# Half of one group's stacking transfers issued by ScalarE instead of SyncE

## The chip, the core and the metric

The kernel runs on one core of a Trainium2 chip. The metric is the device time of one execution in microseconds, median of the timed executions. The engines named here are TensorE (PE, matrix products), VectorE (DVE), ScalarE (ACT), GpSimd (POOL) and SyncE (SP, which only issues transfers here). SyncE and ScalarE can both issue DMA transfers; each has a queue of its own.

## What is computed

A recommendation tower over 512 samples. 26 table rows per sample are gathered, projected and normalised, mixed to 32 rows and normalised again; with one dense row they give 33 vectors, whose pairwise products (the lower triangle) go through a linear layer, a normalisation, and three top layers:

```python
x = layer_norm(dense_t @ Wd.T, gd, bd)
y = layer_norm(jnp.einsum('bnd,ed->bne', sparse_t, Ws), gs, bs)
y = jnp.einsum('bne,pn->bep', y, Wsi)
y = layer_norm(y, gsi, bsi)
y = jnp.swapaxes(y, 1, 2)
T = jnp.concatenate([x[:, None, :], y], axis=1)
Z = jnp.einsum('bnd,bmd->bnm', T, T)
Zflat = Z[:, TRIL_I, TRIL_J]
out = layer_norm(Zflat @ Wl.T, gl, bl)
...
h = jnp.concatenate([z, r_dense_t], axis=1)
h = jnp.maximum(h @ W_top1 + b_top1, 0.0)
h = jnp.maximum(h @ W_top2 + b_top2, 0.0)
y = h @ W_top3
```

## The kernel before

The samples are worked in four groups of 128 (numbers 0 to 3). A group has 26 tiles of gathered rows, taken in 13 pairs (`combine`, line 438) and, two pairs at a time, in quads (`transposes`, `spread_products`, `embT_copy`, `u_sums`, `u_spread`, `scale_rows`), which normalise the gathered rows. Every group also has four blocks of 32 samples, each in two halves: `c_copy` (line 764, ScalarE) takes the mixed rows out of PSUM, `project` (line 457, TensorE) multiplies them by the weights, `y_square` (line 769, ScalarE) squares the result, `y_sums` (line 1088, VectorE) adds it up, `y_spread` (line 775, ScalarE) takes the root and `normalise` (line 1093, VectorE) writes the normalised rows to `T`. `gram_products` (line 477, TensorE) forms the pairwise products in two halves, and `gram_copy` (line 779, ScalarE) copies each half to the tile `gram`; eight such copies make a group, and each raises the semaphore `gram_ready` by one.

The triangle is then folded so that it fills 128 partitions. `stack` (line 351) does that with sixteen SBUF-to-SBUF transfers of 32 KB each (a from 0 to 3, r from 0 to 3), from `gram` to one of two tiles `z`; SyncE issues all sixteen for groups 0, 1 and 2, after `gram_ready` has reached the group's eight copies and after `f_done` says that the flat layer two groups back has read its tile. Each transfer raises `stacked` by 16, so a group is complete at 256. The last group is folded by copies on ScalarE, VectorE and GpSimd instead.

`merge` (line 1104, VectorE) waits for the 256, turns one half (line 1110) and selects between the halves (line 1113) into `zm`. `flat_layer` (line 491, TensorE) multiplies `zm` by the weights of the linear layer (line 503), then a last step (line 507). Its result is normalised (`z_stats`, `f_spread`, `z_normalised`), transposed, scaled, and goes through the top layers `mlp1`, `mlp2` (line 544; line 549 is its product for groups 0 to 2) and `mlp3`.

Every engine has a list of calls of its own, in a fixed order; engines are tied only by semaphores. Up to about the third group the order comes from a clock of ticks with a lag for each call; from there on the order is written out by hand (lines 660 to 738 for TensorE, 920 to 973 for ScalarE, 1189 to 1227 for VectorE). The calls of ScalarE around the change are lines 931 to 942: `gram_copy(end - 4, 1)`, the last copy of group 2's grams; `c_copy(end - 3)` (line 767), two `u_spread` (line 762), `h1_relu(last - 2)` (line 820), `y_square(end - 3)` (line 772), `y_spread(end - 3)` (line 777), `embT_copy(QUADS - 2)` (line 757), `x_columns(last)` (line 788), `c_copy(end - 2)` (line 767) and `h2_relu(last - 2)` (line 834). `last` is 3 and `end` is 15; block `end - 3` is group 3's first. In VectorE's list `merge(last - 1)`, the merge of group 2, stands behind `normalise(end - 2)`; in TensorE's list group 2's flat layer stands behind `gram_products(end - 2, 1)`.

Of the kernel before, what the change touches and what calls it, by code (L numbers as in the profile page):

```python
# [19 lines left out]
PR = 32  # L20
# [7 lines left out]
NG = B // GROUP  # L28
# [4 lines left out]
QUARTERS = GROUP // QS  # L33
# [4 lines left out]
NB = GROUP // 4  # L38
# [80 lines left out]
def wait_if_any(eng, semaphore, value):  # L119

    if value > 0:
        eng.wait_ge(semaphore, value)


def dlrm_tower(nc, t):
    ctx = ExitStack()
    with ctx:
        def sb(name, shape, dt=F32):
            return ctx.enter_context(nc.sbuf_tensor(name, shape, dt))
# [4 lines left out]
        def sem(name):  # L134
            return ctx.enter_context(nc.semaphore(name))
# [21 lines left out]
        z = [sb(f"z{i}", [P, 2, 4, KC, NB]) for i in range(2)]  # L157
# [93 lines left out]
        f_done = sem("f_done")  # L251
# [20 lines left out]
        gram_ready = sem("gram_ready")  # L272
# [37 lines left out]
        stacked = [sem(f"stacked{i}") for i in range(2)]  # L310
# [11 lines left out]
        def folded(g, a, r, columns):  # L322

            at = PR * (a % 2) + KC * r
            of = gram[PR * a:PR * a + PR, g % 2, at:at + KC, columns]
            row, k, column = of.ap
            return bass.AP(of.tensor, of.offset, [row, (NB * (PR - KC - 2 * KC * r), 2), k, column])

        def layer1(g, m):
            return PF[:, P * m:P * m + P] if g < NG - 1 else [*TU, *(c[:, :, :].rearrange("p b c -> p (b c)") for c in PC)][m][:, 0:P]  # L330
# [9 lines left out]
        @block.sync  # L340
        def _(sp):
            sp.dma_start(index_parts[:, :], t["index_parts"]).then_inc(l_ids, 16)
            sp.dma_start(proj_w[:, :], t["proj_w"]).then_inc(l_proj, 16)
            sp.dma_start(bias9[:, 0:E], t["bs"].partition_broadcast(P)).then_inc(l_nine, 16)
            sp.dma_start(sel9[:, :, :], t["sel9"]).then_inc(l_nine, 16)
            sp.wait_ge(gathered[5], 32)
            for dst, src in ((wl, "wl"), (wlx, "wlx"), (gb, "gb"), (sel, "sel"), (gbsi, "gbsi"), (mask, "mask"),
                             (glbl, "glbl"), (w1, "w1"), (b1, "b1"), (w2, "w2"), (b2, "b2"), (w3, "w3")):
                sp.dma_start(dst[tuple(slice(None) for _ in dst.shape)], t[src]).then_inc(l_late, 16)

            def stack(g, samples):

                sp.wait_ge(gram_ready, g * QUARTERS + samples.stop // SLOTS)
                wait_if_any(sp, f_done, g - 1)
                for a in range(4):
                    for r in range(4):
                        sp.dma_start(z[g % 2][PR * r:PR * r + PR, :, a, :, samples], folded(g, a, r, samples)).then_inc(stacked[g % 2], 16)

            for g in range(NG - 1):
                stack(g, slice(0, NB))  # L360

            sp.wait_ge(y_ready, NG)
            sp.dma_start(t["out"].rearrange("b one -> one b"), y_row[:, :]).then_inc(stored, 16)
            sp.wait_ge(stored, 16)
# [376 lines left out]
        def _(act):  # L741
# [13 lines left out]
            def embT_copy(i):  # L755
                act.wait_ge(t_done, i + 1)
                act.activation(embT[:, i % 2, :], TU[i % NTU][:, 0:QUAD], ACT.Copy).then_inc(embT_ready, 1)  # L757

            def u_spread(i):

                act.wait_ge(u_ms_ready, i + 1)
                act.activation(u_sd[:, i % 2, :], u_ms[:, i % 2, :], ACT.Sqrt).then_inc(u_sd_ready, 1)

            def c_copy(m):
                act.wait_ge(c_done, m + 1)
                wait_if_any(act, y_done, m - 1)
                act.activation(cs[:, m % 2, :, :], PC[m % NPC][:, :, :], ACT.Copy).then_inc(cs_ready, 1)

            def y_square(m):
                act.wait_ge(y_done, m + 1)  # L770
                for half in range(2):
                    act.activation(ysq[:, half, :, :], PY[half][:, :, :], ACT.Square,  # L772
                                   scale=float(PR) ** -0.5).then_inc(ysq_ready, 1)

            def y_spread(m):
                act.wait_ge(y_ms_ready, 2 * m + 2)
                act.activation(y_sd[:, m % 2, :, :], y_ms[:, m % 2, :, :], ACT.Sqrt, bias=eps[:, :]).then_inc(y_sd_ready, 1)

            def gram_copy(m, half):
                g, q = m // BLOCKS, 2 * (m % BLOCKS) + half  # L780
                act.wait_ge(z_done, 2 * m + half + 1)
                wait_if_any(act, stacked[g % 2], STACKING * (g // 2))
                act.activation(gram[:, g % 2, :, SLOTS * q:SLOTS * (q + 1)], PZv,  # L783
                               ACT.Copy).then_inc(gram_ready, 1)

            def x_columns(g):
                wait_if_any(act, z_done, g * QUARTERS)
                act.activation(T[:, :, 2 * PR:2 * PR + 2].rearrange("p (b h) s -> p b h s", h=2),
                               xT[:, GROUP * g:GROUP * (g + 1)].rearrange("p (h s b) -> p b h s", h=2, s=2), ACT.Copy).then_inc(xcol_ready, 1)
# [27 lines left out]
            def h1_relu(g):  # L817
                if g < NG - 1:
                    act.wait_ge(h1_sum_ready, g + 1)
                    act.activation(h1[:, :, :], h1[:, :, :], ACT.Relu).then_inc(h1_ready, 1)  # L820
                else:
                    for m in range(H1 // P):
                        act.wait_ge(m1_done, g + m + 1)
                        act.activation(h1[:, m, :], layer1(g, m), ACT.Relu, bias=b1[:, m:m + 1]).then_inc(h1_ready, 1)
# [22 lines left out]
            def wl5_copy():  # L847
                act.wait_ge(w5_done, 1)
                act.activation(wl5[0:ROWS_X, :], PF[0:ROWS_X, :], ACT.Copy).then_inc(wl5_ready, 1)

            def late_stack(g, samples):

                act.wait_ge(gram_ready, QUARTERS * (g + 1))
                for a, r in ACT_PARTS:
                    i = act.activation(z[g % 2][PR * r:PR * r + PR, :, a, :, samples], folded(g, a, r, samples), ACT.Copy)
                i.then_inc(late_stacked, 1)
# [63 lines left out]
            last = NG - 1  # L920
# [9 lines left out]
            embT_copy(QUADS - 3)  # L930
            gram_copy(end - 4, 1)
            c_copy(end - 3)
            u_spread(QUADS - 4)
            u_spread(QUADS - 3)
            h1_relu(last - 2)
            y_square(end - 3)
            y_spread(end - 3)
            embT_copy(QUADS - 2)
            x_columns(last)
            c_copy(end - 2)  # L940
            h2_relu(last - 2)
# [21 lines left out]
            gram_copy(end, 0)  # L963
            gram_copy(end, 1)
            late_stack(last, slice(EARLY, NB))
            h1_relu(last - 1)
            f_spread(last)
# [332 lines left out]
```

## Time and profile before

| | us |
|---|---|
| median of 3 timed runs | 181.1 |
| lowest and highest of them | 179.42, 181.12 |
| span of the profiled execution, first to last instruction | 216.2 |

The page gives the span of the profiled execution and no time around it. Busy shares of that span: TensorE 75%, VectorE 56%, GpSimd 50%, ScalarE 36%. The granted TensorE clock is 0.865 of full speed over the span. Durations below are those of the profiled execution; the start of its span is 0. An issue of a transfer ("SPq", "ACTq") is the time that the issuing engine spends on it, not the time until the data have landed.

### The profile page before, as it was taken

Reading aid. Unit: us, or ns where it says so; the run is one execution under the profiler, and the core shown is the slowest. Engines: PE = TensorE matmul, PEld = TensorE weight load, DVE = VectorE, ACT = ScalarE, POOL = GpSimd, SP = SyncE. Lnnn points to the kernel's source line nnn. Section 1 sums busy time; section 2 is a strip of 40 time slices with the busy share of each in tenths; the row PEclk is TensorE's granted clock in tenths of the full one; section 3 lists DMA queues with packets and bytes.
Section 4 is the critical chain, followed back from the end, with each engine's and each line's share of the span. In section 5 each row is a group of like instructions: output and inputs, shape, how many; then the busy total and the mean of one; then the engine's idle time right before and its main releaser. Section 6 shows DMA issues by size and latency. Waiting matters only on the chain.

```text
span 216.2 us, 3315 instructions
## 1 busy us (share of the span) xinstructions
PE 163.0 (75%) x1189; PEld 110.3 (51%) x1189; DVE 120.7 (56%) x325; ACT 78.7 (36%) x221; POOL 107.9 (50%) x139
## 2 busy tenths in 40 slices
PE   0373406489859698686699689789969999978985
PEld 0171303354645356444275576385649676448574
DVE  1405200997384445766665818559548689876410
ACT  2103001051546354414424234444233655463152
POOL 4777774571665646667545666656755000352000
PEclk9996555859979799969589959799997999999999
DMA  6211891010111101231001112211101011000000
GB/s 210 82 28 26 270 352 25 12 27 15 18 24 20 27 16 21 52 78 37 18 17 23 26 27 55 70 30 24 25 18 28 19 49 33 0 2 3 0 0 0
DMA packets 9730, 9.76 MB, mean 45 GB/s; under 512 B 3666, under 2 KB 7378, under 8 KB 9459
## 3 DMA queue, kind: packets, MB, share of 16 engines
q0 software_dynamic: 3328, 3.41, 8.1%
q1 hardware_dynamic: 5954, 5.18, 7.6%
q10 hardware_dynamic: 432, 0.97, 1.4%
q8 instruction: 9, 0.15, 0.3%
q14 instruction: 7, 0.05, 0.1%
HBM read 7.98 MB, written 0.00 MB: 37 GB/s over the span
## 4 chain that ended last, share of the span: by engine, by line
PE 45%; another core or an unknown queue 17%; DVE 16%; ACT 10%; issue 9%; DMA 2%; SPq 0%; ACTq 0%; DVEq 0%
PE pz L487 7%; PE pc L451 6%; PE pf L503 5%; PE py L472 4%; PE tu L434 4%; PE pf L529 3%; PE tu L424 3%; PE pf L522 3%; DVE y_ms L1091 3%; ACT gram L783 2%; PE py L503 2%; PE py L467 2%; DMA proj_w<-proj_w_dram 2%; PE pf L605 2%
## 5 line engine op out<-in xcount | busy, mean ns | idle before, releaser
L389 POOL DMA_INDIRECT emb<-tables_dram,rows_at x104 | 100.0, 961 | 61.2 <-PE tu L424 26.4
L487 PE MATMUL pz<-T 128*64 128x67 f32 x512 | 24.4, 242 | 9.7 <-ACT gram L783 4.0
L451 PE MATMUL pc<-wbd,emb 128*128 128x192 f32 (+4 forms) x128 | 30.0, 344 | 1.4 <-issue 1.1
L451 PEld LDWEIGHTS pc<-wbd,emb 128*128 128x128 f32 x128 | 20.7, 206 | 20.1 <-issue 17.1
L487 PEld LDWEIGHTS pz<-T 128*64 128x64 f32 x512 | 19.9, 149 | 18.4 <-issue 12.9
L1091 DVE TENSOR_REDUCE y_ms<-ysq 128x16 f32<-128x512 f32 x32 | 20.4, 679 | 12.6 <-ACT ysq L772 12.4
L757 ACT ACTIVATE embT<-tu 128x256 f32<-128x256 f32 x26 | 9.9, 380 | 43.3 <-PE tu L424 31.0
L434 PE MATMUL tu<-mbd,embT 128*128 128x128 f32 x104 | 19.2, 313 | 3.8 <-issue 2.3
L472 PE MATMUL py<-cs,wg 64*128 64x512 f32 x64 | 21.1, 746 | 0.0
L783 ACT ACTIVATE gram<-pz 128x268 f32<-128x268 f32 x32 | 12.5, 389 | 23.7 <-remote 12.6
L1100 DVE TENSOR_TENSOR T<-py,y_r 128x512 f32<-128x512 f32 x32 | 20.6, 687 | 0.6
L424 PE MATMUL tu<-proj_w,emb 128*128 128x128 f32 x52 | 13.0, 326 | 10.2 <-DMA emb<-tables_dram,rows_at 7.8
L772 ACT ACTIVATE ysq<-py 128x512 f32<-128x512 f32 x32 | 17.3, 594 | 8.7 <-PE py L472 6.3
L434 PEld LDWEIGHTS tu<-mbd,embT 128*128 128x128 f32 x104 | 16.1, 214 | 5.1 <-issue 2.6
L1071 DVE TENSOR_TENSOR prod<-tu,emb 128x256 f32<-128x256 f32 x26 | 10.9, 417 | 13.8 <-issue 7.5
L405 POOL COPY z<-gram 32x128 f32<-32x128 f32 x16 | 4.6, 286 | 22.1 <-ACT gram L783 21.4
L424 PEld LDWEIGHTS tu<-proj_w,emb 128*128 128x128 f32 x52 | 7.1, 159 | 14.3 <-DMA emb<-tables_dram,rows_at 9.2
L1082 DVE RECIPROCAL u_r<-u_sd 128x4 f32<-128x4 f32 x26 | 4.5, 172 | 14.5 <-issue 8.4
L503 PE MATMUL pf<-wl,zm 128*128 128x512 f32 x24 | 11.9, 604 | 0.0
L1085 DVE TENSOR_TENSOR emb<-emb,u_r 128x256 f32<-128x256 f32 x26 | 11.1, 429 | 0.9
L1074 DVE TENSOR_REDUCE u_sum<-prod 128x4 f32<-128x256 f32 x26 | 10.9, 420 | 0.9
L529 PE MATMUL pf<-zT,w 128*128 128x128 f32 x72 | 11.0, 308 | 0.0
(142 smaller groups left out, 208.4 us busy)
## 6 DMA issues: line engine op xcount, KB each, us to landing
emb<-tables_dram,rows_at POOLq DMA_INDIRECT x104, 2.4
z<-gram SPq DMA_DIRECT2D x48, 32.0 KB
w<-w_dram SPq DMA_DIRECT2D x1, 1280.0 KB
wl<-wl_dram SPq DMA_DIRECT2D x1, 1024.0 KB
denseT<-denseT_dram ACTq DMA_DIRECT2D x1, 512.0 KB
w<-w_dram SPq DMA_DIRECT2D x1, 512.0 KB
comb_w<-comb_w_dram ACTq DMA_DIRECT2D x1, 311.0 KB, 3.3
sel<-sel_dram SPq DMA_DIRECT2D x1, 240.0 KB
```

The source lines that it names most:

```text
L389: pool.indirect_dma_start(emb[:, 2 * pair + half, :], None, t["tables"], bass.IndirectOffsetOnAxis(ap=rows_at[:, 2 * g + half, j:j + 1], a ...
L424: mm = pe.transpose(TU[i % NTU][:, P * half:P * half + P], emb[:, 4 * i + 2 * half:4 * i + 2 * half + 2, :].rearrange("p t d -> p (t d)"), ...
L434: mm = pe.matmul(TU[i % NTU][:, QUAD + P * half:QUAD + P * half + P], embT[:, i % 2, P * half:P * half + P], mbd[:, :], start=True, stop=True)
L451: mm = pe.matmul(PC[m % NPC][:, :, :].rearrange("p b c -> p (b c)")[:, col:col + n], of, wbd[:, :, :].rearrange("p b c -> p (b c)")[:, at: ...
L472: mm = pe.matmul(PY[half][:, :, :].rearrange("p b c -> p (b c)"), wg[at, :], cs[at, m % 2, :, :].rearrange("p b c -> p (b c)"), start=Fals ...
L487: mm = pe.matmul(PZ[2 * PR * h:2 * PR * h + 2 * PR, ITEMS * b:ITEMS * (b + 1)], of[:, 0:2 * PR], of, start=True, stop=True)
L503: pe.matmul(f_bank(g)[:, :], zm[g % 2][:, k, :, :].rearrange("p a b -> p (a b)"), wl[:, k, :], start=(k == 0), stop=False)
L529: mm = pe.matmul(layer1(g, m), w1[:, c, P * m:P * m + P], zT[:, c, :], start=(c == 0), stop=(c == 2))
L772: act.activation(ysq[:, half, :, :], PY[half][:, :, :], ACT.Square, scale=float(PR) ** -0.5).then_inc(ysq_ready, 1)
L783: act.activation(gram[:, g % 2, :, SLOTS * q:SLOTS * (q + 1)], PZv, ACT.Copy).then_inc(gram_ready, 1)
L1091: dve.tensor_reduce(y_ms[:, m % 2, half, :], ysq[:, half, :, :], AX_X, ALU.add).then_inc(y_ms_ready, 1)
L1100: dve.tensor_tensor(to, PY[half][:, :, :].rearrange("p (b s) c -> p b s c", s=2), y_r[:, m % 2, half, :].rearrange("p (b s) -> p b s", s=2 ...
```

## The change

SyncE's `stack` gets a third argument, the rows a that it is to issue: all four for groups 0 and 1, rows 0 and 1 for group 2. ScalarE gets a call `stack_row` that waits for the same two semaphores and issues the transfers that it is given; four such calls, of two transfers each, stand in its list for rows 2 and 3 of group 2: behind `c_copy(end - 3)`, `h1_relu(last - 2)`, `y_square(end - 3)` and `embT_copy(QUADS - 2)`. The transfers themselves, their tiles and the count that the merge waits for are as before.

```diff
-            def stack(g, samples):
+            def stack(g, samples, rows):
 
                 sp.wait_ge(gram_ready, g * QUARTERS + samples.stop // SLOTS)
                 wait_if_any(sp, f_done, g - 1)
-                for a in range(4):
+                for a in rows:
                     for r in range(4):
                         sp.dma_start(z[g % 2][PR * r:PR * r + PR, :, a, :, samples], folded(g, a, r, samples)).then_inc(stacked[g % 2], 16)
 
             for g in range(NG - 1):
-                stack(g, slice(0, NB))
+                stack(g, slice(0, NB), range(4) if g < NG - 2 else range(2))
...
+            def stack_row(g, a, ranges):
+
+                act.wait_ge(gram_ready, QUARTERS * (g + 1))
+                wait_if_any(act, f_done, g - 1)
+                for r in ranges:
+                    act.dma_start(z[g % 2][PR * r:PR * r + PR, :, a, :, :], folded(g, a, r, slice(0, NB))).then_inc(stacked[g % 2], 16)
+
...
             c_copy(end - 3)
+            stack_row(last - 1, 2, (0, 1))
             u_spread(QUADS - 4)
             u_spread(QUADS - 3)
             h1_relu(last - 2)
+            stack_row(last - 1, 2, (2, 3))
             y_square(end - 3)
+            stack_row(last - 1, 3, (0, 1))
             y_spread(end - 3)
             embT_copy(QUADS - 2)
+            stack_row(last - 1, 3, (2, 3))
             x_columns(last)
             c_copy(end - 2)
             h2_relu(last - 2)
```

## Rows read from the trace of the kernel before

**Rows 1.** The page's chain that ended last: share of the span by engine.

```profile
PE 45%; another core or an unknown queue 17%; DVE 16%; ACT 10%; issue 9%; DMA 2%; SPq 0%; ACTq 0%; DVEq 0%
```

**Rows 2.** The chain in order of time, 160 to 200: start us, us, what.

```profile
172.19 2.05 PE pf L549 x16
...
183.70 2.77 PE pf L503 x6
```

**Rows 3.** Timeline of SyncE's queue, groups 0 and 2: start us, us, engine, line, what.

```profile
87.12 11.17 SPq L357 DMA_DIRECT2D z<-gram  x16
...
170.08 10.18 SPq L357 DMA_DIRECT2D z<-gram  x16
...
171.36 1.24 SPq L357 DMA_DIRECT2D z<-gram  x2
```

**Rows 4.** Line 357, all its issues: ns min/median/max of one, first and last start us.

```profile
L357 SPq DMA_DIRECT2D z<-gram x48: 585/597/1441, 87.1 to 179.7; - x48
```

**Rows 5.** Windows: stretch, its length, busy us (x) of each engine, clock, DMA share, GB/s.

```profile
170.00:184.00 14.00, 13.64 (x136) 9.55 (x135) 12.33 (x33) 8.26 (x24) 0.00 (x0) 1.00 0.16 39
...
181.00:181.50 0.50, 0.50 (x13) 0.38 (x13) 0.50 (x1) 0.50 (x2) 0.00 (x0) 1.00 0.19 46
181.50:182.00 0.50, 0.50 (x16) 0.43 (x13) 0.50 (x3) 0.12 (x2) 0.00 (x0) 1.00 0.00 0
```

**Rows 6.** Timeline of VectorE, 155 to 200.

```profile
172.76 1.27 DVE L1091 TENSOR_REDUCE y_ms<-ysq 128x16 f32<-128x512 f32 x2
...
180.25 1.29 DVE L1100 TENSOR_TENSOR T<-py,y_r 128x512 f32<-128x512 f32 x2
...
181.54 0.72 DVE L1110 STREAM_SHUFFLE zm<-z 128x512 f32<-128x512 f32 x1
182.29 0.73 DVE L1113 COPY_PREDICATED zm<-mask,z 128x512 f32<-128x512 int32 x1
```

**Rows 7.** Timeline of TensorE's products, 166 to 206.

```profile
175.04 0.64 PE L434 MATMUL tu<-mbd,embT 128*128 128x128 f32 x4
...
176.27 0.39 PE L467 MATMUL py<-bias_r,bias_l 64*128 64x512 bf16 x2
...
183.63 2.84 PE L503 MATMUL pf<-wl,zm 128*128 128x512 f32 x6
```

**Rows 8.** Timelines of ScalarE and SyncE near the start: issues of loads.

```profile
1.16 0.46 ACTq L743 DMA_DIRECT2D wdT<-wdT_dram  x1
...
1.22 0.41 SPq L343 DMA_DIRECT2D proj_w<-proj_w_dram  x1
...
22.66 0.42 SPq L349 DMA_DIRECT2D gb<-gb_dram  x1
...
25.02 0.73 SPq L349 DMA_DIRECT2D mask<-mask_dram  x1
```

**Rows 9.** Timeline of ScalarE, 168 to 204; in brackets: idle before it and its releaser.

```profile
169.67 0.39 ACT L783 ACTIVATE gram<-pz 128x268 f32<-128x268 f32 x1 [0.69 <-PE pz L487]
169.96 0.59 ACT L767 ACTIVATE cs<-pc 128x512 f32<-128x512 f32 x1
...
171.42 0.20 ACT L762 ACTIVATE u_sd<-u_ms 128x4 f32<-128x4 f32 x1 [0.78 <-DVE u_ms L1077]
171.53 0.61 ACT L820 ACTIVATE h<-h 128x512 f32<-128x512 f32 x1
172.05 1.06 ACT L772 ACTIVATE ysq<-py 128x512 f32<-128x512 f32 x2
174.06 0.32 ACT L777 ACTIVATE y_sd<-y_ms,eps 128x32 f32<-128x32 f32 x1 [0.95 <-DVE y_ms L1091]
174.50 0.38 ACT L757 ACTIVATE embT<-tu 128x256 f32<-128x256 f32 x1
174.78 0.42 ACT L788 ACTIVATE T<-xT 128x128 f32<-128x128 f32 x1
175.10 0.59 ACT L767 ACTIVATE cs<-pc 128x512 f32<-128x512 f32 x1
```

## Prediction

> **What bounds the kernel now.** I read the page's chain first: TensorE holds 45% of it, and no share belongs to the queue of the stacking transfers [rows 1]. Then the same chain in order of time around the change. From the second layer of group 1 (line 549, 172.19 us) to group 2's flat layer (line 503, 183.70 us) it runs through TensorE alone, instruction behind instruction [rows 2], and TensorE is busy 13.64 of the 14.00 us from 170 to 184 [rows 5]. So in this stretch a microsecond that TensorE is kept waiting is a microsecond of the end, and a microsecond saved elsewhere is worth nothing unless TensorE waited for it.
>
> Next, the queue that the change unloads. SyncE issues group 2's sixteen transfers from 170.08 on in 10.18 us, so the last issue ends at 180.26 [rows 3]; one issue takes 0.597 us in the median [rows 4] and two take 1.24 us [rows 3]. When has the last one landed? The DMA engines still move 46 GB/s in 181.0 to 181.5 and nothing in 181.5 to 182.0 [rows 5]. And who wants it? VectorE's merge of group 2 (lines 1110 and 1113). It starts at 181.54, which is just where the normalisation ahead of it on VectorE ends (180.25 + 1.29 = 181.54), so VectorE did not stand idle for the stack. It ends at 182.29 + 0.73 = 183.02 [rows 6], and TensorE turns to the flat layer only at 183.63 [rows 7]. The stack is just in time on VectorE, and 0.6 us early on TensorE.
>
> **The part taken from SyncE.** Eight issues instead of sixteen end at 170.08 + 8 x 0.64 = 175.2 us, five microseconds sooner. Nothing stands behind them on SyncE but the wait for the output. The merge stays at its place in VectorE's order, behind the normalisation that ends at 181.54, so an earlier stack starts nothing earlier. Gain: none that the rows show on VectorE, and on TensorE none either, for the 0.6 us of slack lies behind the merge. The data are the same bytes in the same number of transfers; two queues feed the same DMA engines, which are busy for 0.16 of this stretch [rows 5].
>
> **The part given to ScalarE.** No row shows ScalarE issuing an SBUF-to-SBUF transfer. Its price is bounded by two rows: ScalarE's own loads at the head, 0.46 us for one [rows 8], and the same transfers on SyncE, 0.62 us [rows 3]. Same shape is the nearer row: 0.62, a pair 1.24. There are four pairs, so 8 x 0.62 = 5.0 us of ScalarE's instruction stream; the added waits (all grams of group 2 copied, group 0's flat layer done) are satisfied at 170.06, when the last gram copy ends [rows 9], and the other one long before.
>
> What of the 5.0 us is felt depends on whether an issue holds up only the calls behind it, or also waits for the call ahead of it. In the rows a ScalarE call starts 0.1 us before the one ahead ends (the copy of line 767 at 169.96, the gram copy ending at 170.06 [rows 9]), so the engine does not empty between calls. I take it that a pair is issued while the call ahead of it is still running. The walk, with old times in brackets, all from [rows 9] for ScalarE and [rows 7] for TensorE:
>
> - Pair 1: 170.08 to 171.32, beside the copy of line 767. The square roots behind it (line 762) come at 171.34 and 171.45 (the second came at 171.42), so h1_relu ends at 172.17 (172.14): 0.03 late for TensorE.
> - Pair 2: 171.58 to 172.82, beside h1_relu. y_square 172.84 to 173.90 (172.05 to 173.11): 0.8 late. VectorE's two y_sums, 0.64 each, begin at 173.4 (172.76 [rows 6]) and end at 174.7.
> - Pair 3 lies beside y_square and y_sums. y_spread 174.72 to 175.04 (174.06), embT 174.95 to 175.33 (174.50 to 174.88).
> - Pair 4: 174.97 to 176.21. x_columns 176.23, c_copy 176.55 to 177.14 (175.10 to 175.69): 1.45 late.
> - TensorE: spread_products wants embT and starts at 175.37 (175.04), 0.33 late. The projection of line 467 wants c_copy: 177.17 (176.27), 0.9 late. From there everything is 0.9 late together, since ScalarE and VectorE now wait for TensorE, and TensorE has no idle time left in which to catch up before the flat layer, whose length doesn't change.
>
> That is the upper end of this reading: +0.9 us. With 0.44 us for an issue (near the head's 0.46) the same walk puts c_copy's end at 176.38 and the projection at 176.41: +0.14. If the calls behind a pair are also handed to the engine before they can run, so that pairs follow one another without waiting for the calls between them, pair 4 is over at 175.2, c_copy ends at 176.2 and the loss is again about 0.1. No row tells these apart; I take the middle of 0.1 and 0.9, +0.5 us. That uses up the cover: c_copy had 176.27 - 175.69 = 0.58 us of slack before the projection.
>
> The Trainium skill has a rule on just this point: in "Perfetto Trace Analysis", "Per-engine timelines", an activation is pushed into a wait queue and the sequencer goes on, while a DMA instruction occupies the sequencer until its descriptors are made. By it the loss would lie near the lower end; the overlap of 0.1 us in [rows 9] agrees with it, and no row shows an issue among ScalarE's calls.
>
> **The sum against the times.** The span of the profiled execution is 216.2 us; the page gives no time around it. The median of the three timed runs is 181.1, so the profiled execution is 35.1 us longer, and no row says where. I carry the difference over unscaled, since in this stretch TensorE works without gaps at a granted clock of 1.00 [rows 5], that is at 2.4 GHz, and has nothing to be shortened: 216.2 + 0.5 = 216.7 for the span, 181.1 + 0.5 = 181.6 for the median. One per cent is 1.8 us, about what a measurement of this kernel can tell from no change.
>
> **Rivals.**
> 1. Slower: an issue on ScalarE begins only when the call ahead has ended. Then pair 1 runs from 170.55 (end of the copy, 169.96 + 0.59), h1_relu ends at 172.6, pair 2 at 173.85, y_square at 174.9, pair 3 at 176.15, embT at 176.8, pair 4 at 178.05, c_copy at 179.0, and the projection is 2.7 us late: 183.8 us. It decides as soon as c_copy is over 0.58 us late. For it: no row shows an issue beside a running call. Against it: the calls themselves overlap.
> 2. Slower still: two queues that issue at once take turns, so that each issue costs 1.24 us while SyncE has work. Pair 1 ends at 172.56, h1_relu at 173.4, pair 2 at 175.3, pair 3 at 177.8, pair 4 (alone) at 179.3, c_copy at 180.2: 4.0 us late, 185.1 us. Against it: at the head ScalarE's issue of 0.46 us runs beside SyncE's of 0.41, and SyncE alone at 22.66 takes 0.42 [rows 8]. The Trainium skill, "Perfetto Trace Analysis", "DMA Instruction — HWDGE", says that the descriptor generator is shared and locked by one sequencer at a time; by that rule this rival would be the forecast, but the two overlapping issues of [rows 8] speak against any turn-taking that shows at that size.
> 3. Faster: in the timed executions SyncE issues more slowly and the merge does wait. SyncE's issues of 0.73 us exist [rows 8], and group 0's sixteen took 11.17 us [rows 3]. The stack has 0.6 us of slack before TensorE, so it decides from 0.64 + 0.6 / 16 = 0.68 us an issue. At 0.73 the stack lands 16 x 0.09 = 1.5 us later, TensorE waits 0.9, and the change takes that away for 0.1 to 0.5 of its own: 180.3 to 180.7 us. For more than 1% the issue would have to take 0.8. For it: the merge starts within hundredths of the landing. Against it: nothing in the profile makes SyncE slower when it isn't profiled.
> 4. No effect at all: ScalarE's pairs fit wholly into its idle time (0.95 us before y_spread and smaller ones [rows 9]): 181.1. This lies inside the forecast's range.
>
> **How the numbers follow.** The forecast with rival 4: 0.62, own range 181.1 to 182.0. Rival 1: 0.20. Rival 2: 0.06. Rival 3: 0.12. Nearly all of the first and most of the last are within 1%; a scatter of the measurement (179.42 to 181.12 in three runs) moves some of each over the line. Faster by over 1%: 0.11, from rival 3 and the scatter. Within 1%: 0.62. Slower by over 1%: 0.27, from rivals 1 and 2. The range, 179.7 to 184.1, takes in rival 3 with some scatter and rival 1; it leaves out rival 2 and a larger gain.
>
> **What would show it.** Right: SyncE's issues of group 2 end near 175; eight issues stand on ScalarE's queue between 170 and 176.5, some of them while a call is running; h1_relu moves by under 0.1, y_square by up to 0.8 and the projection of line 467 by 0.1 to 0.9 relative to the gram copy at 169.67; the merge still follows the normalisation without a gap; the flat layer is late by what the projection is. Wrong: issues that begin only at the end of a call and a projection late by over 2 us (rival 1); issues of over 1 us on both queues (rival 2); a merge that starts earlier against the normalisation, or a flat layer that comes closer to the gram copy (rival 3).

## The result, and the profile after

The changed kernel takes 181.85 us (median of 22 runs, 180.57 to 184.13) against 181.13 us for the kernel before (22 runs, 179.42 to 182.42). The ratio is 1.0052 with a 95% interval of 1.0031 to 1.0074: 0.0052 x 181.13 = 0.9 us slower, between 0.6 and 1.3; the medians lie 0.72 us apart. Ratios here are formed without the runs that took over 1.5% longer than the fastest of their kernel, medians with them, so the two can differ. The loss lies within the 1% band, and the median inside the forecast's own range (181.1 to 182.0), 0.25 us above the time predicted.

The profiled execution of the changed kernel has a span of 180.9 us, not 216. A second trace of the kernel before (the first experiment) has 180.6. So the two kernels are compared below by a common mark, the start of the last gram copy of group 2, after which ScalarE's first added issue comes: 133.20 us in the changed kernel, 133.87 in the second trace of before, 169.67 in the first [rows 9]. An offset is a start minus that mark.

The page of the changed kernel has ScalarE's queue in the chain that ended last, where it had 0% [rows 1]:

```profile
PE 55%; DVE 15%; POOL 11%; ACT 6%; issue 6%; DMA 4%; ACTq 2%; POOLq 0%
```

The timeline of the changed kernel (start us, us, engine, line, what; in brackets the idle time before it and its releaser, where the word "issue" stands for time in which the engine waited for nothing that the profile shows), first ScalarE with its queue, then TensorE, VectorE and SyncE's queue. Line 856 is the added issue; VectorE's lines are eleven higher than before (1121 is the merge, 1111 the normalisation):

```profile
133.20 0.39 ACT L783 ACTIVATE gram<-pz 128x268 f32<-128x268 f32 x1 [0.69 <-PE pz L487]
...
133.62 1.52 ACTq L856 DMA_DIRECT2D z<-gram  x2
135.19 0.30 ACT L762 ACTIVATE u_sd<-u_ms 128x4 f32<-128x4 f32 x2 [1.11 <-DVE u_ms L1088]
135.33 0.59 ACTq L856 DMA_DIRECT2D z<-gram  x1
135.40 0.61 ACT L820 ACTIVATE h<-h 128x512 f32<-128x512 f32 x1
135.96 0.62 ACTq L856 DMA_DIRECT2D z<-gram  x1
136.62 0.60 ACT L772 ACTIVATE ysq<-py 128x512 f32<-128x512 f32 x1 [0.61 <-issue]
136.73 0.61 ACTq L856 DMA_DIRECT2D z<-gram  x1
...
137.37 0.62 ACTq L856 DMA_DIRECT2D z<-gram  x1
138.56 0.32 ACT L777 ACTIVATE y_sd<-y_ms,eps 128x32 f32<-128x32 f32 x1 [0.86 <-DVE y_ms L1102]
138.62 0.59 ACTq L856 DMA_DIRECT2D z<-gram  x1
138.79 0.36 ACT L757 ACTIVATE embT<-tu 128x256 f32<-128x256 f32 x1
139.25 0.64 ACTq L856 DMA_DIRECT2D z<-gram  x1
139.93 0.43 ACT L788 ACTIVATE T<-xT 128x128 f32<-128x128 f32 x1 [0.78 <-issue]
140.26 0.58 ACT L767 ACTIVATE cs<-pc 128x512 f32<-128x512 f32 x1
...
136.06 2.05 PE L549 MATMUL pf<-h,w 128*128 128x128 f32 x16 [0.68 <-issue]
...
140.90 0.39 PE L467 MATMUL py<-bias_r,bias_l 64*128 64x512 bf16 x2 [0.33 <-ACT cs L767]
...
148.25 2.84 PE L503 MATMUL pf<-wl,zm 128*128 128x512 f32 x6
...
144.88 1.29 DVE L1111 TENSOR_TENSOR T<-py,y_r 128x512 f32<-128x512 f32 x2
146.09 0.72 DVE L1121 STREAM_SHUFFLE zm<-z 128x512 f32<-128x512 f32 x1
...
133.62 5.33 SPq L357 DMA_DIRECT2D z<-gram  x8
```

Read it from the top. Issues run while a call is running: the third starts at 135.33 and h1_relu at 135.40, the fifth lies in y_square. What is behind a transfer's issue waits: y_square, with all its inputs there, starts at 136.62, just behind the second pair (135.96 + 0.62 = 136.58), with 0.61 us of idle put down to "issue", where in the first trace of before it followed h1_relu without a gap [rows 9]; x_columns stands behind the last pair with 0.78. The copy of line 767 then comes at 140.26, and the projection of line 467, which had no idle time before it [rows 7], waits 0.33 us for it. SyncE is done at 133.62 + 5.33 = 138.95 instead of ten microseconds after it began [rows 3]; the merge starts at 146.09 all the same, at the end of the normalisation.

The same marks in the second trace of the kernel before (timeline; ScalarE, TensorE, VectorE):

```profile
133.87 0.39 ACT L783 ACTIVATE gram<-pz 128x268 f32<-128x268 f32 x1 [0.69 <-PE pz L487]
...
140.60 0.39 PE L467 MATMUL py<-bias_r,bias_l 64*128 64x512 bf16 x2
...
147.96 2.84 PE L503 MATMUL pf<-wl,zm 128*128 128x512 f32 x6
...
144.57 1.29 DVE L1100 TENSOR_TENSOR T<-py,y_r 128x512 f32<-128x512 f32 x2
145.79 0.72 DVE L1110 STREAM_SHUFFLE zm<-z 128x512 f32<-128x512 f32 x1
```

Offsets of four marks in every trace, each a start minus the mark above, and the timed ratio (the kernels of the experiments have other line numbers; the instructions are the same):

| kernel | second layer (549) | projection (467) | flat layer (503) | statistics (f_bn) | ratio, 95% |
|---|---|---|---|---|---|
| before, first trace | 2.52 | 6.60 | 13.96 | 19.15 | |
| before, second trace | 2.53 | 6.73 | 14.09 | 19.29 | 0.9972 (0.9925 to 1.0018) |
| changed | 2.86 | 7.70 | 15.05 | 20.25 | 1.0052 (1.0031 to 1.0074) |
| all sixteen on ScalarE | 3.97 | 12.17 | 21.19 | 26.39 | 1.0374 (1.0316 to 1.0433) |
| first pair alone | 2.85 | 7.03 | 14.39 | 19.59 | 1.0012 (0.9979 to 1.0045) |
| last pair alone | 2.53 | 7.43 | 14.78 | 19.98 | 1.0038 (0.9998 to 1.0077) |
| SyncE's eight later | 2.68 | 7.50 | 16.12 | 21.66 | 1.0108 (1.0033 to 1.0182) |
| two pairs in idle places | 2.68 | 6.75 | 14.11 | 19.30 | 1.0036 (0.9999 to 1.0072) |
| two extra transfers, SyncE | 2.53 | 6.77 | 14.75 | 20.30 | 1.0072 (1.0008 to 1.0136) |

Against the second trace of before, the changed kernel is 0.33 us late at the second layer, 0.97 at the projection, 0.96 at the flat layer and 0.96 at the statistics. The whole loss is there by the projection, and nothing gives it back. It agrees with the 0.9 us of the timed runs. The two traces of the kernel before differ by 0.13 to 0.14 us from the projection on (against the first, the changed kernel is 1.10 us late there), so an offset is good to about that.

### The profile page after: what moved, and what is told of

Read it like the earlier page. It is cut to its first block, busy times and chain, and to the rows that moved or that the text cites. A ratio compares the mean times of both kernels' runs of the same rounds, so it can differ in the third digit from the quotient of the medians.

```text
span 180.9 us, 3319 instructions
## 1 busy us (share of the span) xinstructions
PE 150.2 (83%) x1189; PEld 103.0 (57%) x1189; DVE 119.8 (66%) x325; ACT 79.6 (44%) x221; POOL 108.1 (60%) x139
## 3 DMA queue, kind: packets, MB, share of 16 engines
q10 hardware_dynamic: 1072, 1.24, 2.1%
## 4 chain that ended last, share of the span: by engine, by line
PE 55%; DVE 15%; POOL 11%; ACT 6%; issue 6%; DMA 4%; ACTq 2%; POOLq 0%
POOL emb L389 11%; PE pz L487 10%; PE pc L451 7%; PE py L472 6%; PE pf L503 6%; PE tu L434 5%; DVE y_ms L1102 3%; PE pf L522 3%; PE tu L424 3%; DMA emb<-tables_dram,rows_at 2%; PE py L467 2%; PE py L503 2%; PE pf L529 2%; DVE T L1111 2%; PE pf L605 2%
## 5 line engine op out<-in xcount | busy, mean ns | idle before, releaser
L451 PE MATMUL pc<-wbd,emb 128*128 128x192 f32 (+4 forms) x128 | 28.9, 335 | 0.8 <-DVE emb L1096 0.8
L451 PEld LDWEIGHTS pc<-wbd,emb 128*128 128x128 f32 x128 | 20.2, 201 | 16.3 <-issue 13.8
L487 PE MATMUL pz<-T 128*64 128x67 f32 x512 | 22.6, 231 | 6.0 <-DVE T L1111 5.0
L487 PEld LDWEIGHTS pz<-T 128*64 128x64 f32 x512 | 18.1, 139 | 14.2 <-issue 6.7
L424 PE MATMUL tu<-proj_w,emb 128*128 128x128 f32 x52 | 12.5, 306 | 11.5 <-DMA emb<-tables_dram,rows_at 11.5
L434 PE MATMUL tu<-mbd,embT 128*128 128x128 f32 x104 | 17.9, 297 | 0.6 <-ACT embT L757 0.5
L472 PE MATMUL py<-cs,wg 64*128 64x512 f32 x64 | 17.9, 639 | 0.0
L434 PEld LDWEIGHTS tu<-mbd,embT 128*128 128x128 f32 x104 | 15.1, 202 | 1.7 <-ACT embT L757 1.1
L767 ACT ACTIVATE cs<-pc 128x512 f32<-128x512 f32 x16 | 9.5, 591 | 3.0 <-PE pc L451 3.0
```

The lines of the kernel that those rows point to most:

```text
L424: mm = pe.transpose(TU[i % NTU][:, P * half:P * half + P], emb[:, 4 * i + 2 * half:4 * i + 2 * half + 2, :].rearrange("p t d -> p (t d)"), ...
L434: mm = pe.matmul(TU[i % NTU][:, QUAD + P * half:QUAD + P * half + P], embT[:, i % 2, P * half:P * half + P], mbd[:, :], start=True, stop=True)
L451: mm = pe.matmul(PC[m % NPC][:, :, :].rearrange("p b c -> p (b c)")[:, col:col + n], of, wbd[:, :, :].rearrange("p b c -> p (b c)")[:, at: ...
L472: mm = pe.matmul(PY[half][:, :, :].rearrange("p b c -> p (b c)"), wg[at, :], cs[at, m % 2, :, :].rearrange("p b c -> p (b c)"), start=Fals ...
L487: mm = pe.matmul(PZ[2 * PR * h:2 * PR * h + 2 * PR, ITEMS * b:ITEMS * (b + 1)], of[:, 0:2 * PR], of, start=True, stop=True)
```

## The experiments

Theory A: ScalarE's stream of instructions stands still for about 0.62 us an issue, so what is behind a pair comes late, and the projection with it. Theory B: the loss comes from two queues that issue and move data at once. The timed ratios of the experiments have intervals of 0.3 to 0.8% to either side, so the offsets decide where a few tenths of a microsecond matter.

**The kernel before, again.** No edit.

> The kernel before, unchanged, for a trace whose span is near the timed median (the first one's was 216.2 us) and for the scatter. Both theories: ratio 1.000 within 0.002, span near 180. In the trace the projection of line 467 comes 6.60 us after the last gram copy of group 2 starts, the flat layer 13.96 us after it, as in the first trace; if the longer span lay in this stretch instead, these would be shorter.

Measured: ratio 0.9972 (0.9925 to 1.0018), span 180.6 us, projection at 6.73 and flat layer at 14.09. The stretch is the same to 0.13 us in a span that is 35.6 us shorter: the mark itself comes 169.67 - 133.87 = 35.8 us earlier, so the long span of the first trace lay wholly ahead of this stretch. Carrying the difference over unscaled was right.

**All sixteen on ScalarE.**

```diff
-                stack(g, slice(0, NB), range(4) if g < NG - 2 else range(2))
+                stack(g, slice(0, NB), range(4) if g < NG - 2 else range(0))
...
-            stack_row(last - 1, 2, (0, 1))
+            stack_row(last - 1, 0, (0, 1, 2, 3))
...
-            stack_row(last - 1, 2, (2, 3))
+            stack_row(last - 1, 1, (0, 1, 2, 3))
...
-            stack_row(last - 1, 3, (0, 1))
+            stack_row(last - 1, 2, (0, 1, 2, 3))
...
-            stack_row(last - 1, 3, (2, 3))
+            stack_row(last - 1, 3, (0, 1, 2, 3))
```

> ScalarE issues all sixteen, four at each of the four places; SyncE issues none. Theory A (ScalarE's instruction stream stands still for 0.62 us an issue, beside the one call already running): four issues take 2.48 us, h1_relu is 1.3 us late, y_square 3.4, the second c_copy and with it the projection 5.4 us late; 181.1 + 5.3 = 186.4 us, ratio about 1.029. Theory B (the loss comes from two queues that issue and move data at once): with one queue silent the loss is no more than with the change, ratio 1.000 to 1.005.

Measured: the second layer is 1.44 us late, the projection 12.17 - 6.73 = 5.44 us late, as theory A had it (5.4); with SyncE silent theory B allowed no more than the change itself costs. Timed it is 1.0374, that is 6.8 us, more than the 5.3 expected. The rest is told by two views. The timeline of this kernel (ScalarE's queue and TensorE):

```profile
132.84 2.63 ACTq L856 DMA_DIRECT2D z<-gram  x4
...
138.97 1.92 ACTq L856 DMA_DIRECT2D z<-gram  x3
...
136.38 2.05 PE L549 MATMUL pf<-h,w 128*128 128x128 f32 x16 [1.79 <-ACT h L820]
...
141.58 1.23 PE L434 MATMUL tu<-mbd,embT 128*128 128x128 f32 x4 [2.18 <-ACT embT L757]
...
144.58 0.61 PE L467 MATMUL py<-bias_r,bias_l 64*128 64x512 bf16 x2 [0.50 <-ACT cs L767]
```

And its windows (stretch, length, busy us (x) of PE, PEld, DVE, ACT, POOL, then granted clock, DMA share, GB/s):

```profile
140.00:142.00 2.00, 0.42 (x2) 0.43 (x3) 1.17 (x5) 0.59 (x2) 0.00 (x0) 0.85 0.20 49
142.00:144.00 2.00, 2.00 (x8) 1.57 (x7) 1.88 (x5) 0.38 (x2) 0.00 (x0) 0.50 0.20 49
144.00:146.00 2.00, 1.50 (x7) 0.65 (x6) 0.60 (x2) 1.14 (x5) 0.00 (x0) 0.50 0.07 16
146.00:148.00 2.00, 2.00 (x16) 0.85 (x14) 0.42 (x1) 1.05 (x2) 0.00 (x0) 0.50 0.00 0
148.00:150.00 2.00, 2.00 (x24) 1.43 (x22) 1.22 (x3) 1.33 (x5) 0.00 (x0) 0.95 0.00 0
```

TensorE waited 1.79 us for h1_relu and 2.18 us for embT, and the granted clock then read 0.50, that is 1.2 GHz, from 142 to 148 us. The four products of line 434 took 1.23 us where they take 0.64 [rows 7]. Between projection and flat layer this kernel loses another 7.10 - 5.44 = 1.66 us; that stretch holds nothing else new. So waits on TensorE can cost more than their own length. In the changed kernel the waits are 0.68 us at the second layer (0.34 in the second trace of before) and 0.33 at the projection, and its clock is 1.00 throughout the stretch.

**The first pair alone.** In this kernel, in the next and in "two pairs in idle places", SyncE issues all that ScalarE does not; the diffs show ScalarE's part alone.

```diff
             c_copy(end - 3)
             stack_row(last - 1, 2, (0, 1))
...
             h1_relu(last - 2)
-            stack_row(last - 1, 2, (2, 3))
             y_square(end - 3)
-            stack_row(last - 1, 3, (0, 1))
             y_spread(end - 3)
             embT_copy(QUADS - 2)
-            stack_row(last - 1, 3, (2, 3))
```

> Only the first of the four pairs stays on ScalarE, the other fourteen transfers go back to SyncE. Theory A: the two roots behind it and h1_relu are 0.3 us late as in the trace of the changed kernel, later calls are not held; the projection is 0.3 late: 181.4 us, ratio 1.002. Theory B: while that pair overlaps with SyncE's issues the same holds, 0.2 to 0.3.

Measured: second layer 0.32 us late, projection 0.30, flat layer 0.30. The timed ratio, 1.0012 (0.9979 to 1.0045), can't tell 0.3 us from nothing. The pair takes 1.51 us, as in the changed kernel (1.52). Line 858 is the issue, in the view of one line (ns min/median/max, first and last start):

```profile
L858 ACTq DMA_DIRECT2D z<-gram x2: 695/740/784, 131.1 to 131.8; - x2
```

**The last pair alone.**

```diff
             c_copy(end - 3)
-            stack_row(last - 1, 2, (0, 1))
...
             h1_relu(last - 2)
-            stack_row(last - 1, 2, (2, 3))
             y_square(end - 3)
-            stack_row(last - 1, 3, (0, 1))
             y_spread(end - 3)
             embT_copy(QUADS - 2)
             stack_row(last - 1, 3, (2, 3))
```

> Only the last of the four pairs stays on ScalarE, behind embT_copy. Theory A: h1_relu and y_square are as before; x_columns and c_copy are late by 0.6 to 1.0, of which 0.58 is slack: the projection is 0 to 0.45 late, 181.1 to 181.6 us. Theory B: a quarter of the loss, 0.2 us, without a shift of c_copy.

Measured: the projection is 0.70 us late, more than either theory gave; the timed ratio of 1.0038 is 0.7 us. The timeline of this kernel (ScalarE, TensorE; lines 759, 769 and 469 are embT, c_copy and the projection):

```profile
135.80 0.38 ACT L759 ACTIVATE embT<-tu 128x256 f32<-128x256 f32 x1
135.86 1.51 ACTq L858 DMA_DIRECT2D z<-gram  x2
...
137.75 0.58 ACT L769 ACTIVATE cs<-pc 128x512 f32<-128x512 f32 x1
...
138.39 0.39 PE L469 MATMUL py<-bias_r,bias_l 64*128 64x512 bf16 x2 [0.75 <-ACT cs L769]
```

The direction is theory A's (c_copy is shifted, the projection waits for it). Two sizes were off: the pair took 1.51 us instead of 1.24, and it began when embT began, not already with y_spread. One pair at a bad place costs 0.70 of the 0.97 us that four cost.

**SyncE's eight later.**

```diff
                 wait_if_any(sp, f_done, g - 1)
+                if g == NG - 2:
+                    sp.wait_ge(xcol_ready, NG)
                 for a in rows:
```

> As the changed kernel, but SyncE's eight issues wait until x_columns has run, so behind ScalarE's last pair: the two queues never issue at once. Theory A: ScalarE's pairs take as long as before or little less (1.24 in place of 1.52 us for the first), the projection is 0.8 to 1.1 late; SyncE's last transfer now lands about when the merge wants it or up to 0.9 later, so the flat layer is 0.8 to 1.4 late: 181.9 to 182.5 us. Theory B: the pairs shrink to where the projection is late by less than 0.3.

Measured: the projection is 7.50 - 6.73 = 0.77 us late with no overlap between the queues, 0.20 less than in the changed kernel. So about 0.2 us of the loss is a matter of two queues at once (the first pair takes 1.33 us here instead of 1.52, which says the same; 0.20 alone is little more than the 0.13 by which two traces differ), and 0.77 us is ScalarE's own stream. Theory B, which allowed less than 0.3, falls. The total came out worse than expected, 1.0108, because the stack now came late. The timeline (SyncE's queue, the merge's first instruction):

```profile
138.72 6.24 SPq L359 DMA_DIRECT2D z<-gram  x8
...
143.19 1.78 SPq L359 DMA_DIRECT2D z<-gram  x1
...
146.25 0.01 DVE L1123 LOAD_MASK_SELECT zm<-z  x1 [1.81 <-DMA z<-gram]
```

Seven of the issues took 0.6 us and the eighth 1.78, with no other queue at work; why, no run shows. Issues as long are in every trace: the second of group 0's stack took 1.22 to 1.82 us in all nine (in the kernel before it is the 1441 ns of [rows 4]). The merge waited 1.81 us, of which 1.2 are that issue, and the flat layer is 2.03 us late.

**Two pairs in idle places.**

```diff
             c_copy(end - 3)
-            stack_row(last - 1, 2, (0, 1))
...
             h1_relu(last - 2)
-            stack_row(last - 1, 2, (2, 3))
             y_square(end - 3)
             stack_row(last - 1, 3, (0, 1))
             y_spread(end - 3)
             embT_copy(QUADS - 2)
-            stack_row(last - 1, 3, (2, 3))
             x_columns(last)
             c_copy(end - 2)
             h2_relu(last - 2)
+            stack_row(last - 1, 3, (2, 3))
```

> Four transfers on ScalarE, in two pairs at places where it stood idle for 0.9 us: one behind y_square(end - 3), one behind h2_relu(last - 2); twelve on SyncE. Theory A: a pair of 1.24 us that begins when the call ahead of it begins its last 0.6 us ends within the idle time, so the projection is not late: 181.0 to 181.3 us, ratio 0.999 to 1.001, although half as many issues stand on ScalarE as with the change. Theory B: half of the loss stays, 181.5 us.

Measured: projection at 6.75, flat layer at 14.11, statistics at 19.30, each within 0.02 us of the kernel before, although four issues stand on ScalarE. (The second layer is 0.15 us late because h1_relu is, and h1_relu began ahead of the first issue.) The timed ratio, 1.0036 (0.9999 to 1.0072), neither shows nor excludes a loss; the medians, 181.08 and 181.32, lie the other way round. By the trace theory A holds and half of a loss (theory B) does not. The timeline of ScalarE and its queue (774 is y_square, 769 the copy, 836 h2_relu):

```profile
135.07 0.69 ACTq L858 DMA_DIRECT2D z<-gram  x1
135.30 1.06 ACT L774 ACTIVATE ysq<-py 128x512 f32<-128x512 f32 x2
135.80 0.82 ACTq L858 DMA_DIRECT2D z<-gram  x1
137.27 0.32 ACT L779 ACTIVATE y_sd<-y_ms,eps 128x32 f32<-128x32 f32 x1 [0.91 <-DVE y_ms L1102]
...
138.34 0.59 ACTq L858 DMA_DIRECT2D z<-gram  x1
138.35 0.59 ACT L769 ACTIVATE cs<-pc 128x512 f32<-128x512 f32 x1
138.83 0.37 ACT L836 ACTIVATE h<-pf,b 128x128 f32<-128x128 f32 x1
138.96 0.86 ACTq L858 DMA_DIRECT2D z<-gram  x1
```

The pair written behind y_square starts 0.23 us before y_square does, and the pair written behind h2_relu 0.49 us before h2_relu (138.34 against 138.83), even before the copy that stands ahead of h2_relu (138.35). An issue waits for the calls ahead of it to be handed over, not for them to run or even to begin. It also shows the other half of the answer: SyncE is done 2.5 us sooner here at no cost, and the kernel is no faster.

**Two extra transfers on SyncE.**

```diff
+                if g == NG - 2:
+                    for r in range(2):
+                        sp.dma_start(spare[PR * r:PR * r + PR, :, :, :], folded(g, 0, r, samples)).then_inc(spared, 16)
                 for a in range(4):
```

The tile `spare`, the semaphore `spared` and a wait for it at the program's end are left out of this diff.

> The kernel before, with two more transfers of the same size to a tile that nobody reads, ahead of group 2's sixteen on SyncE: the stack lands 1.25 us later. If the merge of the kernel before is just in time (start within 0.1 us of the landing, 0.6 us of slack before TensorE): the merge starts 1.2 us later, the flat layer 0.6 us later, 181.7 us. If the stack landed well before the merge: no change, 181.1 us. If the merge was already held: the full 1.2 us, 182.3 us.

Measured: the flat layer is 14.75 - 14.09 = 0.66 us late, as worked out. The timeline (SyncE's queue, the merge, TensorE's flat layer, the statistics; lines 362, 1116, 509, 1131):

```profile
134.82 10.19 SPq L362 DMA_DIRECT2D z<-gram  x16
...
146.33 0.01 DVE L1116 LOAD_MASK_SELECT zm<-z  x1 [1.18 <-DMA z<-gram]
...
147.87 1.55 PE L509 MATMUL pf<-wl,zm 128*128 128x512 f32 x3 [0.55 <-DVE zm L1119]
...
153.42 0.69 DVE L1131 BATCH_NORM_STATS2 f_bn<-pf 128x6 f32<-128x512 f32 x1
```

The last issue ends at 134.82 + 10.19 = 145.01 and the merge starts 1.32 us later. Put on the kernel before, where the last issue ends at an offset of 0.42 + 10.18 = 10.60, that is 11.92: just where its merge starts (145.79 - 133.87). So in the kernel before the stack lands in the very moment in which VectorE is ready for it. An earlier stack wins nothing; a later one holds VectorE at once, and TensorE beyond its 0.6 us of slack. At the statistics the loss has grown to 1.01 us, since VectorE's own calls behind the merge are late too and the statistics stand behind them; the expectation had counted only TensorE's 0.6 us of slack. Timed: 1.0072 (1.0008 to 1.0136).

None of these versions beats the kernel before.

## Why the prediction was right

- **Nothing to gain from SyncE.** Right. SyncE ended 5.33 us after it began (5.1 worked out), the merge did not move against the normalisation, and the kernel with two pairs in idle places had the earlier stack for nothing and was no faster.
- **Price of an issue on ScalarE: 0.62 us.** Right for six of the eight (0.59 to 0.64). The first two took 0.70 and 0.79, so that pair 1 lasted 1.52 us instead of 1.24. h1_relu was therefore 0.34 us late where the walk had 0.03, and y_square 1.04 (3.42 after the mark against 2.38 [rows 9]) where it had 0.8. The first issue on ScalarE's queue after the loads took 0.70 us in all six kernels that have one; the second 0.78 to 0.82 where SyncE was issuing, and 0.61 where it was silent (1.33 for the pair). A later one took 0.86, the last of the kernel with two pairs in idle places.
- **A pair is issued while the call ahead runs.** Right, and the trace shows more: an issue can start before the call ahead does. What holds it back is a call ahead of it in the list whose semaphore has still to come. In the kernel with the last pair alone it began 0.06 us after embT; in the changed kernel, where embT's input was already there when y_spread began, it began with y_spread, before embT.
- **The walk's end, +0.9 us.** Measured +0.97 at the projection, of which 0.20 goes away where SyncE is silent. The last pair, c_copy and the projection came in the order and by the way that was worked out. That the size fits so well is in part luck: against the first trace of before, on which the walk was made, the projection is 1.10 us late, and two errors of the walk work against each other. Pair 1 took 0.28 us more, and the last pair began 0.17 us before embT, where the walk had it 0.02 behind.
- **The middle of 0.1 and 0.9.** This is the step that was mis-sized: +0.5 us forecast, +0.97 in the trace, +0.9 by the timed ratio. The 0.1 had two grounds. One was an issue of 0.44 us; none on ScalarE took less than 0.59. The other was pairs that follow one another without waiting for the calls between them. They can't: y_spread waits for VectorE's sums until 138.56, and the last pair stood behind that wait and began at 138.62. The walk had the last pair behind that wait, and its own end should have been taken: +0.9, not +0.5. The Trainium skill's rule ("Perfetto Trace Analysis", "Per-engine timelines"), that an activation is pushed into a wait queue and the sequencer goes on, had spoken for the lower end. The trace agrees for calls whose inputs are there and disagrees where a semaphore has still to come. The overlap of 0.1 us in [rows 9], which the prediction took as a sign for the rule, lies between two calls whose inputs were there, and so could not tell.
- **Rival 1 (issues begin only when the call ahead has ended, +2.7 us)** falls by the timeline: six of the eight begin while a call is running, and the projection is under 1 us late. **Rival 2 (turn-taking, +4.0 us)** falls: pairs 2 and 3 took 1.25 and 1.26 us beside SyncE's issues; only the first pair's second issue was longer, by 0.17 us, and SyncE's eight took 5.33 us instead of 5.1. **Rival 3 (the merge waited in the timed runs)** falls: the merge was just in time, and an earlier stack brought nothing. The 11.17 us of group 0's sixteen [rows 3], which spoke for it, held one issue of 1.44 us, not sixteen slower ones. **Rival 4 (no effect)** falls by the interval of the ratio.

## What to carry to other kernels

An issue of such a transfer (32 KB, SBUF to SBUF) cost ScalarE 0.59 to 0.86 us of its instruction stream, in whatever place it was written. Written ahead of a call that has to wait at least as long anyway, it hides in that wait; written behind such a call it starts only when the wait is over, and shifts every call behind it until somebody on the critical path waits. Before moving issues off a queue, look whether the consumer of the transfers waits at all; here VectorE took its data in the moment in which they landed, so that more speed was worth nothing, while a stack that came 1.3 us later cost the flat layer 0.66. Where a walk through the rows gives a number, keep it; averaging it with a reading that no row bore out made the forecast worse here.

## What was not expected of the hardware

An issue can start before calls that stand ahead of it in the same engine's list, by up to 0.49 us here, but not past a call whose semaphore has still to come: it then began 0.06 us after that call. With all sixteen issues on ScalarE, TensorE waited 1.79 and 2.18 us and its granted clock read 0.50 for the next 6 us, which cost 1.66 us beside the waits. One issue on SyncE took 1.78 us instead of 0.6, with no other queue issuing, and the second issue of group 0's stack took 1.22 to 1.82 us in every trace; neither is explained. The profiled span of one kernel was 216.2 us once and 180.6 us once, with the difference wholly ahead of group 2's last gram copy.
